# A decoder layer on one core: attention products moved one group later, one of the maxima products moved within its group

## The chip, the cores and the metric

The kernel runs on one core of a Trainium2 chip (trn2). The time is device microseconds of one execution, from launch to the last store; a measurement is repeated and its median given. The profile is of one execution of its own. Below, "us" is microseconds. PE is TensorE (matrix products), DVE is VectorE, ACT is ScalarE, POOL is GpSimd, SP is the engine that issues most DMAs here.

## The reference

Two sequences of 256 tokens, width 256 (512 tokens in all), pass through one decoder layer:

```python
x = layernorm(x + self_attention(x))        # 16 heads of 16, latents of 64, rotary half appended to q and k
x = layernorm(x + cross_attention(x, ctx))  # 16 heads, scores against 512 context rows of width 64
x = layernorm(x + moe(x))                   # 8 experts of 128, two per token, and a shared expert
```

The cross attention multiplies several weights of a head one after the other:

```python
q_hk  = (hidden_q @ Wq.T).reshape(b, s, H, K)
q_big = einsum('bshk,hkq->bshq', q_hk, w_kc_q)
q_r   = einsum('bshq,hqr->bhsr', q_big, W_qr)
k_r   = einsum('bld,hdr->bhlr', kv_rope, W_kr)
scores = einsum('bhsr,bhlr->bhsl', q_r, k_r)
```

The kernel multiplies these four weights with each other first, once for each head, so that a head's scores are x times one 256x64 matrix times the rotated context. These are the weight products that the change moves.

## The kernel before

All five engines run programs written out by hand; each engine executes its own list in order, and semaphores (`wait_ge`, `then_inc`) tie the lists together. What follows is about the first 70 us: the self attention.

**Groups.** The self attention is cut into 8 groups (`NGRP`), i = 0 to 7: four for each sequence, each of four heads (two pairs, pr = 0 and 1). The loop `for i in range(NGRP + 1): for j in range(4)` stands in the PE, ACT and DVE programs alike; a slot (i, j) says when a step is issued. For group i, in slots (i, 0) and (i, 2), PE computes the scores of a pair (`attn_max`, L587), DVE takes the row maxima (L1361), splits them in two parts (`max_split`, L1372 to L1376), PE transposes them (`attn_maxT`, L599, slot (i+1, 0)), and DVE adds them into the rows of `QS` (`max_rows`, L1383), which increments `mT_sb`. Two groups later PE computes the transposed scores (`attn_exp`, L613), ACT exponentiates (L1100); three groups later comes the product with the values (`attn_pv`, L629), four groups later the sum of the exponentials (`attn_sum`, L639) and on DVE its reciprocal (`attn_norm`, L1332 and L1335).

**Spread products.** Before group 2 (the heads of the third quad) can start, the operands `KS` and `QS` for pairs 4 to 7 are built: `late_stack(0)` to `late_stack(3)` (L548), in the slots `LATE_STACKS = [(0, 3), (1, 0), (1, 1), (1, 2)]`. All four write PSUM banks 2 and 3, so each waits until the one before is evacuated: 0 by ACT (KS, L1081), 1 by DVE (KS, L1300), 2 by ACT (QS, L1083), 3 by DVE (QS, L1302). The first `attn_max` of group 2 waits for all of them (`stack_act`, `stack_dve` at 4).

**Weight products.** For each of the 8 pairs of heads p (`NPAIR`) there are three steps on PE, each followed by an evacuation on ACT: E(p) (`step_E`, L681, 4 matmuls, loads as weights `wE`), G(p) (`step_G`, L694, 8 matmuls, needs E(p)), M(p) (`step_M`, L709, 8 matmuls, needs G(p)). Their slots come from `product_slots`; before the change they are:

```
group 0: E2 M0 | G1    | E3 M1 | G2        group 4:        |       | M6 | G7
group 1: E4 M2 | G3    | E5 M3 | G4        group 5:        |       | M7 |
group 2:       | E6    | M4    | G5
group 3:       | E7    | M5    | G6
```

M(p) and the transposed maxima of `attn_maxT` share PSUM bank 7. So `attn_maxT(i)` waits for the evacuations of the M before it (`M_out`), and M(p) waits for `max_rows` of the transpose before it (`mT_sb`). The weights of pairs 2g and 2g+1 come by three DMAs (`ld_wg[g]`); only E waits for them.

**Filler.** `keep_busy(n, 4)` issues n bf16 matmuls of 256 columns into bank 4 whose results nobody reads (L508). Group 1 has 8 of them in slot (1, 0) and 3 in each of (1, 1), (1, 2) and (1, 3).

**Next to it.** U products (`step_U`, L719) follow in slots (6, 1), (7, 1), (8, 0) and (8, 1); (6, 1) waits for all E evacuations. The output projection `attn_proj` in slot (7, 2) uses bank 6 after the last G. After group 8 come 18 rounds of cross attention and then the experts; they take M(p) from `M_sb`, and start after all M are evacuated.

Of the kernel before, what the change touches and what calls it, by code (L numbers as in the profile page):

```python
# [34 lines left out]
NPAIR = NH // 2  # L35
# [7 lines left out]
NGRP = 2 * NQUAD  # L43
# [5 lines left out]
def product_slots():  # L49
    slots = {}  # L50
    for p in range(NPAIR):
        fast = p < 4
        i, j = (p // 2, 2 * (p % 2)) if fast else (p - 2, 1)
        for step, q, at in [("E", p + 2, j), ("M", p, j if fast else j + 1), ("G", p + 1, j + 1 if fast else j + 2)]:
            if q < NPAIR:
                slots.setdefault((i, at), []).append((step, q))
    return slots


PRODUCTS = product_slots()  # L60
SH = 792
LAG = 2
# [6 lines left out]
def decoder_layer(nc, xT_in, pk_in, rope_in, spread_in, wE_in, wcT_in, wq_in, bv_up, xn_in, bo, wop_in, wu_in, sh_in,  # L69
                  kv_in, w13_in, w2_in, out):  # L70
    stack = ExitStack()
    with stack:
# [3 lines left out]
        def sem(name):  # L76
            return stack.enter_context(nc.semaphore(name))
# [140 lines left out]
        v_sb = sem("v_sb")  # L218
# [11 lines left out]
        mT_sb = sem("mT_sb")  # L230
# [13 lines left out]
        M_out = sem("M_out")  # L244
# [257 lines left out]
        def _(pe):  # L502
            def bank(k):
                return ps[:, k, :]

            def keep_busy(count, k):
                for _ in range(count):
                    pe.matmul(ps[:, k, 0:2 * P], busy[:, 0:P], busy[:], start=True, stop=True)  # L508
# [65 lines left out]
            def attn_max(i, pr):  # L574

                b, g = i // NQUAD, i % NQUAD
                n = 2 * i + pr
                if i in (0, 2) and pr == 0:
                    pe.wait_ge(stack_act, 2 + i)
                    pe.wait_ge(stack_dve, 2 + i)  # L580
                if n >= 1:
                    pe.wait_ge(max_sb, n)
                for u in range(2):
                    t = 2 * b + u
                    for par in range(2):
                        r = slice(64 * par, 64 * par + KROWS)
                        mm = pe.matmul(ps[:, par, u * SEQ:(u + 1) * SEQ], QS[r, 2 * g + pr, t * P:(t + 1) * P],  # L587
                                       KS[r, 2 * g + pr, b * SEQ:(b + 1) * SEQ], start=True, stop=True)
                mm.then_inc(max_ps, 1)

            def attn_maxT(i):

                if i == 0:
                    pe.wait_ge(consts, 2)
                pe.wait_ge(mpad_sb, i + 1)
                pe.wait_ge(M_out, 2 if i == 0 else min(NPAIR, i + 3))
                for pr in range(2):
                    for u in range(2):
                        mm = pe.transpose(ps[:, 7, pr * SEQ + u * P:pr * SEQ + (u + 1) * P], mpad[:, i % 2, u, pr, :], ident[:])  # L599
                mm.then_inc(mT_ps, 1)  # L600
# [97 lines left out]
            def step_M(p):  # L698

                pe.wait_ge(G_out, p + 1)  # L700
                if p == 0:
                    pe.wait_ge(rot_sin, 2)
                if p >= 1:
                    pe.wait_ge(M_out, p)
                if p in (2, 4, 5, 6, 7):
                    pe.wait_ge(mT_sb, max(1, p - 2))
                for c in range(2):
                    for k in range(2):
                        mm = pe.matmul(ps[:, 7, c * P + DC * k:c * P + DC * k + DC], wq[:, 2 * p + k, c * P:(c + 1) * P],  # L709
                                       G_sb[:, p % 2, DC * k:DC * k + DC], start=True, stop=True)  # L710
                mm.then_inc(M_ps, 1)
# [14 lines left out]
            step_G(0)  # L726
            for i in range(NGRP + 1):
                for j in range(4):
                    if i < NGRP and j % 2 == 0:
                        attn_max(i, j // 2)  # L730
                    if i >= ALAG and j % 2 == 0:
                        attn_exp(i - ALAG, j // 2)
                    if i >= 1 and j == 0:
                        attn_maxT(i - 1)
                    if (i, j) == (0, 2):
                        values(2)
                    if (i, j) in LATE_STACKS:
                        late_stack(LATE_STACKS.index((i, j)))
                    if i == 1:
                        if j == 0:  # L740
                            pe.wait_ge(v_sb, 2)
                        keep_busy(8 if j == 0 else 3, 4)
                    if i >= ALAG + 2 and j == 0:
                        attn_sum(i - ALAG - 2)
                    if i >= ALAG + 1 and j == 2:
                        attn_pv(i - ALAG - 1)
                    if i in (2, 3) and j == 1:
                        context_T(i - 2)
                    for step, p in PRODUCTS.get((i, j), []):
                        if step == "E":  # L750
                            step_E(p)
                        elif step == "M":
                            step_M(p)
                        else:
                            step_G(p)
                    if i == 6 and j == 1:
                        pe.wait_ge(E_out, NPAIR)
                        step_U(0, bank(5))
                    if i == 7 and j == 1:
                        pe.wait_ge(U_out, 1)  # L760
                        step_U(1, bank(5))
                    if i == 7 and j == 2:
                        pe.wait_ge(G_out, NPAIR)
                        attn_proj(0, ps[:, 6, 0:D], range(NQUAD))
                    if i == 7 and j == 3:
                        pe.wait_ge(U_out, 2)
                        attn_proj(1, ps[:, 5, 0:D], range(NQUAD))
                    if i == 8 and j < 2:
                        if j == 0:
                            pe.wait_ge(max_sb, 2 * NGRP)  # L770
                        step_U(2 + j, bank(j))
                    if i == 8 and j >= 2:
                        normed_T(0, x1, j - 2, 8 - j)
# [498 lines left out]
        def _(dve):  # L1272
# [24 lines left out]
            def stack_out(kq, count, pairs):  # L1297
                dve.wait_ge(stack_ps, count)
                if kq == 0:
                    v.tensor_scalar(KS[:, pairs, :], ps[:, 2:4, :], one_rows, None, ALU.add).then_inc(stack_dve, 1)  # L1300
                else:
                    v.tensor_copy(QS[:, pairs, :], ps[:, 2:4, :]).then_inc(stack_dve, 1)  # L1302
# [62 lines left out]
            def max_split(i):  # L1365

                dve.wait_ge(max_sb, 2 * i + 2)
                if i == 0:
                    dve.wait_ge(mpad_zero, 1)
                if i >= 2:  # L1370
                    dve.wait_ge(mT_ps, i - 1)
                v.tensor_copy(mhi[:, i % 2], mneg[:, i % 2]).then_inc(mhi_sb, 1)  # L1372
                dve.wait_ge(mhi_sb, i + 1)
                at = mpad[:, i % 2].rearrange("p u r (h c) -> p u (r h) c", h=2)
                v.tensor_copy(at[:, :, :, KROWS], mhi[:, i % 2].bitcast(F32))
                v.tensor_tensor(at[:, :, :, KROWS + 1], mneg[:, i % 2], mhi[:, i % 2].bitcast(F32), ALU.subtract).then_inc(mpad_sb, 1)  # L1376
# [8 lines left out]
            for i in range(NGRP + 1):  # L1385
                for j in range(4):
                    if i < NGRP and j % 2 == 0:
                        attn_max(i, j // 2)
                    if i == 0 and j in (0, 2):
                        values(j // 2)  # L1390
                    if i == 0 and j in (1, 2):
                        rotated_lo(j - 1)
                    if i >= 1 and j == 0:
                        max_rows(i - 1)
                    if (i, j) == LATE_STACKS[1]:
                        stack_out(0, 4, slice(6, 8))
                    if (i, j) == LATE_STACKS[3]:
                        stack_out(1, 6, slice(6, 8))
                    if i < NGRP and j == 2:
                        max_split(i)  # L1400
                    if i >= ALAG + 2 and j == 0:
                        attn_norm(i - ALAG - 2)
                    if i in (2, 3) and j == 1:
                        context_lo(i - 2)
                    if i == NGRP - 1 and j >= 2:
                        if j == 2:
                            dve.wait_ge(xbo, NT)
                        norm_stats(0, j - 2, ps[:, 8 - j, 0:D], x_nat)
                    if i == NGRP and j >= 2:
                        norm_apply(0, j - 2, x1)  # L1410
# [249 lines left out]
```

## Time and profile before

| what | value |
|---|---|
| time, median of 3 runs | 255.16 us (255.13 to 256.3) |
| time of the profiled execution | 255.44 us |
| its span, first to last instruction | 253.7 us |
| PE matmul busy | 238.6 us, 94% of the span |
| DVE busy | 194.2 us, 77% |
| ACT busy | 120.6 us, 48% |
| POOL busy | 119.8 us, 47% |
| TensorE clock granted, mean | 0.993 of full |

The span is the time between the first and last instruction of the profiled execution; what lies around it is 1.7 us. The busy share of PE counts overlapping records of a pipelined engine, so the time that a step takes of PE is better read from the distance between the start of its first matmul and the start of the next step.

### The profile page before, as it was taken

The page shows a single profiled execution, that of the slowest core. Times are in us where ns is not written, and L with a number is a line of the kernel's source. Part 1 is how long each engine was busy: PE and PEld are TensorE (multiplying, and loading weights), DVE is VectorE, ACT ScalarE, POOL GpSimd, SP SyncE. Part 2 cuts the span into 40 slices and gives each one's busy share as a digit, 9 for nine tenths or more (in the row PEclk, how much of TensorE's full clock was granted, in tenths as well). Part 3 has the DMA queues.
Part 4 walks back from the last instruction along what each step waited for, and adds up shares of the span by engine and source line. Part 5 has one row for each costly group of instructions (what it writes and reads, how often), then busy time and mean ns, then how long its engine had stood idle before and what let it go on. Part 6 is the DMA issues. An engine that isn't in the chain of part 4 may idle for free.

```text
span 253.7 us, 4411 instructions
## 1 busy us (share of the span) xinstructions
PE 238.6 (94%) x1581; PEld 172.7 (68%) x1581; DVE 194.2 (77%) x348; ACT 120.6 (48%) x253; POOL 119.8 (47%) x170
## 2 busy tenths in 40 slices
PE   7989999978999999999899999999999999999991
PEld 4468797755656557675667776668776777778870
DVE  1377578799874899769889999995857895886685
ACT  2555358655566355454366554454344434513360
POOL 7297300000025528757666666784465646502353
PEclk9999999999999999999999999999999999999997
DMA  6999970000000660000000000000000000000002
GB/s 240 331 268 264 402 281 0 4 1 3 0 3 1 123 125 3 0 0 0 4 0 0 4 0 0 4 0 0 3 0 0 0 4 0 0 3 0 0 3 83
DMA packets 4501, 13.66 MB, mean 54 GB/s; under 512 B 513, under 2 KB 1281, under 8 KB 4353
## 3 DMA queue, kind: packets, MB, share of 16 engines
q1 hardware_dynamic: 4048, 11.29, 13.8%
q0 software_dynamic: 432, 2.10, 3.8%
q8 instruction: 13, 0.21, 0.4%
q14 instruction: 8, 0.06, 0.1%
HBM read 14.43 MB, written 0.52 MB: 59 GB/s over the span
## 4 chain that ended last, share of the span: by engine, by line
PE 70%; DVE 16%; DMA 5%; issue 2%; ACT 2%; SPq 2%; POOL 1%; POOLq 0%
PE ps L854 10%; PE ps L807 6%; PE ps L868 5%; PE ps L834 5%; PE ps L835 5%; PE ps L808 5%; DMA wq<-in_wq 5%; PE ps L791 5%; DVE rcp L1332 3%; PE ps L934 3%; PE ps L647 3%; DVE mneg L1361 3%; PE ps L841 2%; DVE xmneg L1423 2%; PE ps L709 2%
## 5 line engine op out<-in xcount | busy, mean ns | idle before, releaser
L1195 ACT ACTIVATE probs<-ps 128x512 f32<-128x512 f32 x64 | 38.0, 597 | 57.0 <-PE ps L835 56.0
L1423 DVE TENSOR_REDUCE xmneg<-ps 128x1 f32<-128x512 f32 x64 | 43.1, 688 | 18.0 <-PE ps L808 17.7
L454 POOL TENSOR_TENSOR psums<-psums,probs 128x512 f32<-128x512 f32 x32 | 41.2, 1287 | 11.2 <-ACT probs L1195 8.5
L450 POOL TENSOR_TENSOR psums<-probs 128x512 f32<-128x512 f32 x16 | 20.5, 1281 | 34.2 <-ACT probs L1195 22.6
L807 PE MATMUL ps<-KA,QA 128*128 128x512 f32 x64 | 30.1, 470 | 2.1 <-DVE xmneg L1423 2.1
L854 PE MATMUL ps<-probs,kv_dup 128*64 128x256 f32 x256 | 31.1, 385 | 0.0
L1441 DVE RECIPROCAL xrcp<-ps 128x256 f32<-128x256 f32 x16 | 28.0, 1751 | 1.1 <-PE ps L841 1.0
L1361 DVE TENSOR_REDUCE mneg<-ps 128x4 f32<-128x1024 f32 x16 | 19.6, 1224 | 9.5 <-PE ps L587 9.1
L834 PE MATMUL ps<-QA,KA 128*128 128x512 f32 x64 | 26.0, 406 | 0.0
L398 POOL TENSOR_TENSOR rstd<-mv,eps_col 128x1 f32<-128x1 f32 x12 | 2.3, 188 | 49.5 <-DVE mv L1349 49.2
L835 PE MATMUL ps<-QB,KB 68*128 68x512 f32 x64 | 25.4, 397 | 0.0
L808 PE MATMUL ps<-KB,QB 68*128 68x512 f32 x64 | 25.3, 395 | 0.0
L854 PEld LDWEIGHTS ps<-probs,kv_dup 128*64 128x64 f32 x256 | 17.0, 136 | 11.2 <-ACT probs L1195 3.0
L1100 ACT ACTIVATE probs<-ps 128x512 f32<-128x512 f32 x32 | 17.3, 593 | 10.6 <-PE ps L613 10.5
L807 PEld LDWEIGHTS ps<-KA,QA 128*128 128x128 f32 x64 | 12.0, 188 | 11.8 <-DVE xmneg L1423 5.8
L791 PE MATMUL ps<-x1T,M_sb 128*128 128x256 f32 x64 | 16.4, 380 | 0.5 <-ACT x1T L1145 0.5
L868 PE MATMUL ps<-U_sb,ctxn 128*128 128x256 f32 x64 | 16.5, 380 | 0.2 <-DVE ctxn L1446 0.2
L1187 ACT ACTIVATE QA<-ps 64x256 fp32r<-64x256 f32 x32 | 12.1, 378 | 8.8 <-PE ps L791 8.4
L1416 DVE TENSOR_TENSOR QB<-ps,QA 64x256 fp32r<-64x256 f32 x32 | 13.3, 416 | 3.7 <-ACT QA L1187 3.2
L1223 ACT ACTIVATE QB<-ps,own_rows 4x256 fp32r<-4x256 f32 x32 | 13.1, 455 | 4.9 <-PE ps L818 4.6
L834 PEld LDWEIGHTS ps<-QA,KA 128*128 128x128 f32 x64 | 12.1, 190 | 3.3 <-issue 0.8
L1332 DVE RECIPROCAL rcp<-sums 128x256 f32<-128x256 f32 x8 | 14.0, 1748 | 0.3 <-ACT sums L1107 0.2
(163 smaller groups left out, 464.1 us busy)
## 6 DMA issues: line engine op xcount, KB each, us to landing
wu<-in_wu SPq DMA_DIRECT2D x4, 640.0 KB, 9.8
wq<-in_wq SPq DMA_DIRECT2D x4, 512.0 KB, 13.9
wcT<-in_wcT SPq DMA_DIRECT2D x4, 384.0 KB, 12.6
wE<-in_wE SPq DMA_DIRECT2D x4, 320.0 KB, 11.5
w13T<-in_w POOLq DMA_DIRECT2D x1, 1024.0 KB, 7.8
x1T<-in_xT SPq DMA_DIRECT2D x1, 512.0 KB, 3.7
kvp<-in_kv POOLq DMA_DIRECT2D x1, 512.0 KB, 6.1
x_nat<-in_xn SPq DMA_DIRECT2D x1, 512.0 KB, 19.6
```

Source lines behind the costliest of these rows:

```text
L454: g.tensor_tensor(psums[:, s, :], psums[:, s, :], probs[:, s, kc, :], ALU.add).then_inc(xadd_sb, 1)
L791: mm = pe.matmul(ps[:, query_bank(n), 0:SEQ], M_sb[:, c, p, :], x1T[:, c, b * SEQ:(b + 1) * SEQ], start=(c == 0), stop=(c == 1))
L807: pe.matmul(o, QA[:, s, hh, q], KA[:, b * LK:(b + 1) * LK], start=True, stop=False)
L808: pe.matmul(o, QB[:, s, hh, q], KB[:, b * LK:(b + 1) * LK], start=False, stop=True).then_inc(xmax_ps, 1)
L834: pe.matmul(o, KA[:, k0:k0 + P], QA[:, s, :, :], start=True, stop=False)
L835: pe.matmul(o, KB[:, k0:k0 + P], QB[:, s, :, :], start=False, stop=True).then_inc(xexp_ps, 1)
L854: mm = pe.matmul(ps[DC * hh:DC * hh + DC, 4 + n % 2, 0:SEQ], kv_dup[:, NKC * b + kc, 0, :], probs[:, n % 2, kc, hh * SEQ:(hh + 1) * SEQ], ...
L868: mm = pe.matmul(o, ctxn[:, p, t * P:(t + 1) * P], U_sb[:, p, :], start=(p == 0 and t < 2), stop=(p == NPAIR - 1))
L1195: a.activation(probs[:, n % 2, kc, :], ps[:, 2 + u % 2, :], ACT.Exp).then_inc(xexp_sb, 1)
L1361: v.tensor_reduce(mneg[:, i % 2, :, 2 * pr:2 * pr + 2].rearrange("p u h -> p h u"), ps[:, 0:2, :].rearrange("p h (u k) -> p h u k", u=2), ...
L1423: v.tensor_reduce(xmneg[:, n % 4, qt, hh:hh + 1], ps[:, u % 2, :], AX.X, ALU.max, negate=True).then_inc(xmax_sb, 1)
L1441: v.reciprocal(xrcp[:, n % 2, :], ps[:, 4 + n % 2, SEQ:2 * SEQ]).then_inc(xrcp_sb, 1)
```

## The change

The table of slots gets its slow pace from pair 3 on instead of pair 4:

```
group 0: E2 M0 | G1    | E3 M1 | G2        group 4:        | E7    | M5 | G6
group 1: E4 M2 | G3    |       |           group 5:        |       | M6 | G7
group 2:       | E5    | M3    | G4        group 6:        |       | M7 |
group 3:       | E6    | M4    | G5
```

The waits that keep bank 7 in order are adapted: `attn_maxT(i)` waits for M up to i+1, and M(p) from p = 2 on waits for `max_rows` of group p-2. The second `attn_max` of group 1 is issued in slot (1, 1), ahead of the third spread product `late_stack(2)`, instead of in slot (1, 2). The filler of group 1 is one call of 8 matmuls in slot (1, 3). On DVE `max_split` of a group stands ahead of the evacuation of the last spread product.

```diff
--- before.py
+++ after.py
@@ -49,8 +49,8 @@
 def product_slots():
     slots = {}
     for p in range(NPAIR):
-        fast = p < 4
-        i, j = (p // 2, 2 * (p % 2)) if fast else (p - 2, 1)
+        fast = p < 3
+        i, j = (p // 2, 2 * (p % 2)) if fast else (p - 1, 1)
         for step, q, at in [("E", p + 2, j), ("M", p, j if fast else j + 1), ("G", p + 1, j + 1 if fast else j + 2)]:
             if q < NPAIR:
                 slots.setdefault((i, at), []).append((step, q))
@@ -593,7 +593,7 @@
                 if i == 0:
                     pe.wait_ge(consts, 2)
                 pe.wait_ge(mpad_sb, i + 1)
-                pe.wait_ge(M_out, 2 if i == 0 else min(NPAIR, i + 3))
+                pe.wait_ge(M_out, min(NPAIR, i + 2))
                 for pr in range(2):
                     for u in range(2):
                         mm = pe.transpose(ps[:, 7, pr * SEQ + u * P:pr * SEQ + (u + 1) * P], mpad[:, i % 2, u, pr, :], ident[:])
@@ -702,8 +702,8 @@
                     pe.wait_ge(rot_sin, 2)
                 if p >= 1:
                     pe.wait_ge(M_out, p)
-                if p in (2, 4, 5, 6, 7):
-                    pe.wait_ge(mT_sb, max(1, p - 2))
+                if p >= 2:
+                    pe.wait_ge(mT_sb, p - 1)
                 for c in range(2):
                     for k in range(2):
                         mm = pe.matmul(ps[:, 7, c * P + DC * k:c * P + DC * k + DC], wq[:, 2 * p + k, c * P:(c + 1) * P],
@@ -726,8 +726,10 @@
             step_G(0)
             for i in range(NGRP + 1):
                 for j in range(4):
-                    if i < NGRP and j % 2 == 0:
+                    if i < NGRP and j % 2 == 0 and (i, j) != (1, 2):
                         attn_max(i, j // 2)
+                    if (i, j) == (1, 1):
+                        attn_max(1, 1)
                     if i >= ALAG and j % 2 == 0:
                         attn_exp(i - ALAG, j // 2)
                     if i >= 1 and j == 0:
@@ -736,10 +738,9 @@
                         values(2)
                     if (i, j) in LATE_STACKS:
                         late_stack(LATE_STACKS.index((i, j)))
-                    if i == 1:
-                        if j == 0:
-                            pe.wait_ge(v_sb, 2)
-                        keep_busy(8 if j == 0 else 3, 4)
+                    if (i, j) == (1, 3):
+                        pe.wait_ge(v_sb, 2)
+                        keep_busy(8, 4)
                     if i >= ALAG + 2 and j == 0:
                         attn_sum(i - ALAG - 2)
                     if i >= ALAG + 1 and j == 2:
@@ -1394,10 +1395,10 @@
                         max_rows(i - 1)
                     if (i, j) == LATE_STACKS[1]:
                         stack_out(0, 4, slice(6, 8))
+                    if i < NGRP and j == 2:
+                        max_split(i)
                     if (i, j) == LATE_STACKS[3]:
                         stack_out(1, 6, slice(6, 8))
-                    if i < NGRP and j == 2:
-                        max_split(i)
                     if i >= ALAG + 2 and j == 0:
                         attn_norm(i - ALAG - 2)
                     if i in (2, 3) and j == 1:
```

## Rows read from the trace of the kernel before

**Rows 1.** Chain of waits that ended last: start us, length us, what.
```profile
46.01 1.23 DVE mneg L1361
...
53.52 1.67 DVE rcp L1332
...
59.19 1.67 DVE rcp L1332
```

**Rows 2.** Timeline of PE, group 1: start us, us (first start to last end), what, idle before.
```profile
25.71 0.50 PE L548 MATMUL ps<-dhi,spread 32*128 32x512 f32 x2
...
26.38 1.05 PE L508 MATMUL ps<-busy 128*128 128x256 bf16 x8
27.26 0.60 PE L681 MATMUL ps<-wE 128*96 128x128 f32 x4
27.70 1.00 PE L709 MATMUL ps<-resid,wq 128*128 128x64 f32 x8
28.63 0.50 PE L548 MATMUL ps<-dhi,spread 32*128 32x512 f32 x2
...
30.57 0.50 PE L587 MATMUL ps<-KS,QS 48*128 48x256 f32 x4
31.00 0.50 PE L548 MATMUL ps<-dhi,spread 32*128 32x512 f32 x2
...
32.43 1.00 PE L709 MATMUL ps<-resid,wq 128*128 128x64 f32 x8
33.27 0.49 PE L508 MATMUL ps<-busy 128*128 128x256 bf16 x3
33.60 1.00 PE L694 MATMUL ps<-resid,wcT 96*128 96x64 f32 x8
34.53 0.50 PE L587 MATMUL ps<-KS,QS 48*128 48x256 f32 x4
```

**Rows 3.** Timelines of DVE and then ACT, group 1.
```profile
26.38 0.68 DVE L1383 TENSOR_TENSOR QS<-ps,QS 128x512 fp32r<-128x512 f32 x1
26.98 1.27 DVE L1300 TENSOR_SCALAR KS<-ps,pk 128x1024 fp32r<-128x1024 f32 x1
...
32.25 1.22 DVE L1302 CAST QS<-ps 128x1024 fp32r<-128x1024 f32 x1
...
29.40 1.02 ACT L1083 ACTIVATE QS<-ps 128x1024 fp32r<-128x1024 f32 x1 [0.28 <-PE ps L548]
```

**Rows 4.** Timeline of the DMA queue of SP, and the landing times of the wq transfers.
```profile
7.36 0.43 SPq L312 DMA_DIRECT2D wq<-in_wq x1
...
DMA to landing us min/median/max: 8.2/13.9/18.8
```

**Rows 5.** Timeline of PE, groups 4 to 7.
```profile
46.63 0.60 PE L639 MATMUL ps<-CT,sel 128*128 128x256 f32 x2
47.30 0.50 PE L587 MATMUL ps<-KS,QS 48*128 48x256 f32 x4
...
49.91 1.06 PE L694 MATMUL ps<-resid,wcT 96*128 96x64 f32 x8
51.15 0.50 PE L587 MATMUL ps<-KS,QS 48*128 48x256 f32 x4 [0.18 <-DVE mneg L1361]
...
54.64 1.10 PE L709 MATMUL ps<-resid,wq 128*128 128x64 f32 x8
56.83 0.50 PE L587 MATMUL ps<-KS,QS 48*128 48x256 f32 x4 [1.08 <-DVE mneg L1361]
...
60.20 1.07 PE L629 MATMUL ps<-probs,V 128*32 128x256 f32 x16
62.50 0.50 PE L587 MATMUL ps<-KS,QS 48*128 48x256 f32 x4 [1.23 <-DVE mneg L1361]
```

**Rows 6.** Stretches: bounds us, length, busy us (count) by engine, PEclk granted, DMA share, GB/s.
```profile
56.80:62.50 5.70, 4.45 (x46) 2.67 (x47) 5.48 (x9) 3.41 (x7) 0.00 (x0) 1.00 0.01 3
250.00:253.70 3.70, 0.00 (x0) 0.00 (x0) 1.09 (x2) 0.00 (x0) 0.85 (x3) 0.51 0.22 73
```

## The prediction

> **What bounds the kernel now.** I read the page first, then the chain of waits in order of time, then the timelines of PE, DVE and ACT over the self attention, and last the stretches with the granted clock. The chain shows two regimes. Up to about 46 us nearly every piece of it is a PE piece. From there on it runs through DVE: the maxima at 46.01, then one reciprocal per group, at 53.52 and 59.19, so a group takes 59.19 - 53.52 = 5.67 us whatever PE does [rows 1]. The timeline of PE says the same: in group 1 no row between 25.71 and 34.53 has idle time before it, so each step there pushes the next [rows 2]; in groups 5 and 6 PE sits idle for 1.08 and 1.23 us until DVE has read the scores (56.83 and 62.50) [rows 5]. Work taken off PE in groups 1 to 3 can therefore bring its full length; work put on PE in groups 5 and 6 is free up to about a microsecond each. That is the argument; what follows is whether the waits let it through.
>
> **What is taken from group 1.** I take the PE time of a step as the distance to the next start. E: 27.70 - 27.26 = 0.44. M followed by filler, as M3 is: 33.27 - 32.43 = 0.84; M followed by real work: 28.63 - 27.70 = 0.93. G: 34.53 - 33.60 = 0.93. Three fillers: 33.60 - 33.27 = 0.33; eight: 27.26 - 26.38 = 0.88. A late spread product: 26.38 - 25.71 = 0.67. A maxima product: 31.00 - 30.57 = 0.43 [rows 2]. Group 1 loses E5 (0.44), M3 (0.84), G4 (0.93) and nine of 17 fillers (3 x 0.33 = 0.99): 3.20 us. This is the most the change can bring in group 1.
>
> **What waits appear in it.** I walk group 1 from 26.38, where the second spread product ends and nothing has changed yet.
> - E4 starts at 26.38 and not at 27.26, and ends its slot at 26.82. Its weights must be there: the last of the three transfers of this pair of pairs is issued at 7.36, and even with the longest landing time of the four, 18.8, it is there at 26.2 [rows 4].
> - M2 now waits for `max_rows(0)` on DVE, 26.38 + 0.68 = 27.06 [rows 3]; with a few hundredths for the signal it starts at 27.10. That is the first new wait, 0.28. Slot end 28.03.
> - The second maxima product, 28.03 to 28.46; it waits for the first one's reduction, which is over before `max_rows(0)` begins.
> - The third spread product at 28.46 (the KS evacuation it waits for ends at 26.98 + 1.27 = 28.25 [rows 3]). ACT begins the evacuation 29.40 - 28.63 = 0.77 after the product starts and takes 1.02 [rows 2, 3]: 29.23 to 30.25.
> - G3 from 29.13 to 30.06. The fourth spread product needs ACT's evacuation: 30.30, a second wait of 0.24. DVE evacuates it from 30.30 + 0.77 = 31.07, for 1.22 [rows 3], to 32.29. DVE is free by then: the reduction, 1.23 by [rows 1], starts at about 28.6 and the three tiny instructions of the split follow.
> - The eight fillers end their slot at 30.30 + 0.67 + 0.88 = 31.85. The first maxima product of group 2 waits for DVE: 32.35, a third wait of 0.50.
>
> Group 2 starts at 32.35 in place of 34.53 [rows 2]: 2.18 us earlier. The cross sum agrees: 3.20 - 0.28 - 0.24 - 0.50 = 2.18. The bounds: no waits would give 3.20. If each of the four hand-overs (DVE to PE, PE to ACT, ACT to PE, PE to DVE to PE) took 0.1 more than I allow, it is 1.8.
>
> **Groups 2 and 3** hold the same kinds of steps as before, with p one lower (E5 for E6, M3 for M4, G4 for G5, and so on), and the same waits between them; all of them move together. I cost this at nothing, since as much work leaves each of these groups as enters it. No DMA is issued by a moved step. The queue of SP isn't touched; the U weights and the expert weights come from other places in it and are first needed in group 6.
>
> **Group 4** gets E7 in slot (4, 1) (before, it had no E). Before, the sum product ends at 46.63 + 0.60 = 47.23 and the second maxima product starts at 47.30, when DVE has done the first maxima (46.01 + 1.23 = 47.24) [rows 1, 5]. In the old times E7 runs 47.23 to 47.67 and pushes all behind it by 0.37. The last step of the group (G6 in place of G7) then starts at 49.91 + 0.37 = 50.28 and its slot ends at 51.21; before, the next group's maxima product started at 51.15, released by DVE [rows 5]. DVE takes the product at once, so this loss of 0.06 goes to the end of the kernel. With the full record of G (1.06) it is 0.19. I take 0.10.
>
> **Group 5** gets G7 behind M6. From 54.64 + 0.10: M 0.93, G 0.93, slot end 56.60. DVE releases the next maxima product at 56.83 + 0.10 = 56.93 [rows 5]. Hidden, with 0.33 to spare; with the full records (1.10 and 1.06) it ends at 56.90, just inside. **Group 6** gets M7 behind the product with the values: 60.20 + 0.10 + 1.07 = 61.37, slot end 62.30, full record 62.47, and DVE releases at 62.60 [rows 5]. Hidden again. M7 must also be evacuated before `attn_maxT(6)`; that transpose comes after a maxima product (0.43) and a scores product of group 7, and the evacuation is one ACT instruction over half the columns of the 1.02 one [rows 3]. The cover of both is DVE's 5.67 us per group; if it were gone, G7 and M7 would cost 0.93 each. From group 7 on nothing is changed, and everything there hangs on semaphores of this program, so the shift reaches the end.
>
> **The sum.** 2.18 - 0.10 = 2.1 us. The profiled span would go from 253.7 to 251.6 and the profiled execution from 255.44 to 253.3. That execution lay 0.28 above the median of the runs; against the median, 255.16 - 2.1 = 253.1 us, 0.8% less. What this measurement can tell from no change is about 0.5%, or 1.28 us.
>
> **The rivals.**
> - *A, the forecast:* gain 1.4 to 2.6 us, 252.6 to 253.8. Lower end: hand-overs of 1.8 and the full 0.4 of near misses in groups 4 to 6; upper end: half of the three waits not there. Chance 0.72.
> - *B, the moved products come back in the DVE-bound groups.* For it: three steps are added there, and the spare time is thin (0.33 and 0.30 us). If E7, G7 and M7 all lay on the path, 0.44 + 0.93 + 0.93 = 2.30 us would be paid back and the time would be 255.3; if half of it does, 254.1. Against it: the two idle times of 1.08 and 1.23 us are long enough for a step of 0.93 each [rows 5]. Chance 0.15, of which 0.11 ends within 0.5%.
> - *C, the waits in group 1 are longer, so that the chain of spread products and evacuations, not PE, sets its length.* It does already in my walk (third wait). If the evacuation of the third spread product on ACT came 1 us late, behind other evacuations, the gain would be 1.1 and the time 254.1. Against it: ACT has only E4 and M2 to evacuate before it. Chance 0.04, within 0.5%.
> - *D, the gain is larger,* 2.6 to 3.2 us (252.0 to 252.6): the waits overlap with what is modelled as PE time. Chance 0.04.
> - *E, slower: the clock of TensorE falls in groups 1 to 3,* where nine fillers are gone and three waits appear. Every microsecond of full-speed work takes two at the lower of the two levels (1.2 against 2.4 GHz). From the second wait, 30.30, to the start of group 4, 43.3 (its first maxima product stands 0.5, the record of such a product, ahead of the reduction at 46.01, less 2.2 [rows 1, 2]), lie 13 us of PE-bound work: all of it at the lower level gives 253.1 + 13 = 266 us; 2.1 + 1.28 = 3.4 us of it suffices to be slower by over 0.5%. Against it: a stretch without any filler, 56.80 to 62.50, with 4.45 us busy of 5.70 and a wait of 1.23, was granted 1.00, and the only stretch with a low grant (0.51) is the last 3.7 us, where PE did nothing [rows 5, 6]. The new waits are half a microsecond at most. Chance 0.05.
>
> The Trainium skill speaks for E: its page "TensorE: Matmul & The Clock Gate", section "A second HAM failure mode: psum-queue depth-cycling", says that a PE which idles briefly and often between groups of matmuls, as it cycles through PSUM banks, can swing between the two clock levels. By it this kernel would lose its clock in group 1 and more so in groups 5 and 6, which wait longer and hold no filler. This trace does not agree, since those groups were granted 1.00.
>
> **How the numbers follow.** Faster by over 0.5%: A and D whole and 0.04 of B, 0.80. Within 0.5%: 0.11 of B and C, 0.15. Slower: E, 0.05. The predicted time is A's, 253.1. The range of 252.3 to 254.5 reaches over A into D and to the half-paid case of B and to C; it leaves out E, the full B and the far end of D, under 2 in 10.
>
> **What would show it.** In the profile after: E4 at 26.4 and M2 at about 27.1 with a short wait for DVE L1383; the fourth spread product at about 30.3, released by ACT; the first maxima product of group 2 at 32.3 to 32.5, released by DVE L1302; group 4's first at 43.3 to 43.5; the idle time before the maxima products of groups 6 and 7 shrunk from 1.08 and 1.23 to about 0.3 each, still ended by DVE; reciprocals still 5.67 apart; a granted clock of 1.00 throughout. The prediction is wrong if group 2 starts later than 33.2 (C), if the idle time before those two products is zero and reciprocals are more than 5.7 apart (B), or if a stretch before 50 us has a clock under 1 (E).

## The result and the profile after

| what | before | after |
|---|---|---|
| median of 20 executions | 255.46 us | 254.16 us |
| fastest execution | 255.13 us | 253.17 us |
| ratio, 95% interval | 1 | 0.996 [0.9941, 0.998] |
| profiled execution, its span | 255.44, 253.7 us | 256.40, 254.6 us |
| mean granted clock in it | 0.993 | 0.982 |

The change is faster by 0.4%, half of the 0.8% that were forecast. The median is a poor description of it: the 20 executions are of two kinds. Eleven have a mean granted clock of 0.993 or more and take 253.17 to 254.26 us; nine have 0.987 or less and take 255.03 to 265.76 us. The profiled one is of the second kind. The ratio leaves out two executions that were far off, while the counts below take all of them. Below, an execution has "lapsed" where its mean clock is 0.990 or less, and its clock is "held" otherwise; "the fall" is the moment at which the granted clock goes from 1.00 to 0.50.

The stretches of the changed kernel, columns as in [rows 6]:

```profile
24.00:30.60 6.60, 6.45 (x48) 4.84 (x48) 5.25 (x9) 3.03 (x5) 2.87 (x6) 1.00 1.01 387
30.60:37.40 6.80, 6.72 (x33) 4.91 (x32) 3.98 (x6) 1.99 (x5) 0.77 (x2) 0.50 0.74 295
37.40:64.00 26.60, 25.76 (x260) 19.93 (x258) 22.89 (x37) 18.18 (x42) 0.00 (x0) 1.00 0.01 2
```

For 6.8 us the grant is 0.50, the lower level of 1.2 GHz. It falls at 30.66 us, at the second of the new waits. The timeline of PE in the same execution, against [rows 2] and [rows 5]:

```profile
26.60 0.68 PE L681 MATMUL ps<-wE 128*96 128x128 f32 x4
27.42 1.07 PE L709 MATMUL ps<-resid,wq 128*128 128x64 f32 x8
28.43 0.50 PE L587 MATMUL ps<-KS,QS 48*128 48x256 f32 x4
...
29.52 1.10 PE L694 MATMUL ps<-resid,wcT 96*128 96x64 f32 x8
30.70 0.79 PE L548 MATMUL ps<-dhi,spread 32*128 32x512 f32 x2
31.30 0.62 PE L548 MATMUL ps<-dlo,spread 32*128 32x512 f32 x2
31.85 1.89 PE L508 MATMUL ps<-busy 128*128 128x256 bf16 x8
33.67 0.79 PE L587 MATMUL ps<-KS,QS 48*128 48x256 f32 x4
...
40.16 0.50 PE L587 MATMUL ps<-KS,QS 48*128 48x256 f32 x4
...
57.76 0.50 PE L587 MATMUL ps<-KS,QS 48*128 48x256 f32 x4 [0.18 <-DVE mneg L1362]
...
63.43 0.50 PE L587 MATMUL ps<-KS,QS 48*128 48x256 f32 x4 [0.20 <-DVE mneg L1362]
```

Read it from the top. E4 comes directly after the spread product; M2 comes 0.82 later where E takes 0.44, because of the wait for `max_rows(0)` (first new wait, 0.38); the fourth spread product comes 1.18 after G3 where G takes 0.94, because of the wait for ACT (second new wait, 0.24), and from there each record is longer: the pair of spread records 0.79 and 0.62 where [rows 2] has 0.50, eight fillers 1.82 to the next start against 0.88. Below, G7 and M7 have filled the idle time before the first maxima products of groups 6 and 7: 1.08 and 1.23 in [rows 5], 0.18 and 0.20 now. DVE still ends both.

### The profile page after: what moved, and what is told of

It is laid out like the page before. It is cut to its first block, busy times and chain, and to the rows that moved or that the text cites. A ratio compares the mean times of both kernels' runs of the same rounds, so it can differ in the third digit from the quotient of the medians.

```text
span 254.6 us, 4393 instructions
## 1 busy us (share of the span) xinstructions
PE 242.2 (95%) x1572; PEld 174.8 (69%) x1572; DVE 195.5 (77%) x348; ACT 120.9 (47%) x253; POOL 119.9 (47%) x170
## 4 chain that ended last, share of the span: by engine, by line
PE 77%; DVE 15%; ACT 3%; issue 2%; POOL 1%; POOLq 0%
PE ps L855 10%; PE ps L808 6%; PE ps L869 5%; PE ps L835 5%; PE ps L836 5%; PE ps L809 5%; PE ps L792 5%; PE ps L935 3%; PE ps L647 3%; PE ps L508 3%; DVE rcp L1333 3%; PE ps L587 2%; PE ps L842 2%; DVE xmneg L1424 2%; PE ps L709 2%
```

## The experiments

Fifteen runs follow: eleven new kernels, and again the change, the kernel before and (twice) the second of the new ones. Executions of the kernel before were taken beside them in four sets, 97 in all. Two theories went in. Theory 1: the schedule saves what was predicted, and the clock takes a part back in some executions. Theory 2: the clock is noise common to all versions, and the schedule saves less than predicted.

**Filler back where it was.**
```diff
-                    if (i, j) == (1, 3):
-                        pe.wait_ge(v_sb, 2)
-                        keep_busy(8, 4)
+                    if i == 1:
+                        if j == 0:
+                            pe.wait_ge(v_sb, 2)
+                        keep_busy(8 if j == 0 else 3, 4)
```


> The change, with the 17 filler matmuls of group 1 back where they were (8 in slot (1, 0), 3 in each of the other three). Theory 1 (the products moved save what was predicted, but with the emptier group 1 the TensorE clock falls in a part of the executions, as in the profile of the changed kernel from 30.7 to 37.4 us): with the filler the clock holds; the fillers cost 0.7 us of the gain, since the walk of group 1 then ends at 33.0 in place of 32.35, so about 253.9 us in every execution, with none near 256. Theory 2 (the low clock in that profile is chance and as frequent in any version; the smaller gain comes from waits or from groups 4 to 6): executions scatter as those of the change do, 253.9 to 257, median about 255.

Median 254.03 us (ratio 0.9933 [0.9908, 0.9958]). Ten of 12 executions took 253.64 to 254.42 us; two had a clock of 0.987, at 255.5. So there were fewer lapses (2 of 12 against 9 of 20, a difference that chance could still give), though not none as expected, and the fillers cost some 0.5 us of time. The profiled execution held its clock, so where the two lapsed is not shown.

**Filler in the waits.** The 2 + 2 fillers stand where PE waits, and 12 where it waits for DVE's last evacuation.
```diff
                         elif step == "M":
+                            if (i, j) == (1, 0):
+                                pe.wait_ge(v_sb, 2)
+                                keep_busy(2, 4)
                             step_M(p)
...
+                    if (i, j) == (1, 2):
+                        keep_busy(2, 4)
                     if (i, j) in LATE_STACKS:
...
-                        keep_busy(8, 4)
+                        keep_busy(12, 4)
```


> The change, with filler put into its three new waits: 2 before M2, 2 before the fourth spread product, 12 in place of 8 in slot (1, 3); 16 in all. Theory 1: the clock holds, and since the filler lies in idle time the time is 253.2 us in all executions, 0.9% under before: it beats both kernels. Theory 2: no different from the change, median 254.2 with executions at 256 to 256.6.

Median 253.77 us, ratio 0.9918 [0.9891, 0.9945], six executions from 253.22 to 254.06, clock 0.992 to 0.999. Two further sets of executions follow below.

**The filler edit alone, in the kernel before.** The same diff as the first one, read backwards, applied to the kernel before.

> The kernel before with only the filler edit of the change: 8 in slot (1, 3), none in the other slots of group 1; all products where they were. Theory 1 in the form that missing filler alone makes the clock fall: executions near 254.5 (0.99 us of filler gone from the path, 0.3 us of a new wait before M2) mixed with others 2 to 3 us above. Theory 1 in the form that the waits of the change are needed for it: 254.5 us throughout. Theory 2: 254.5 with the scatter of the kernel before.

Eight of 12 executions took 254.78 to 255.32 us with the clock held; four lapsed, one at 255.87 us and three at 260.82, 273.31 and 273.66, with clocks of 0.976, 0.924 and 0.925. Among the 97 executions of the kernel before, one was as late as these three (271.51). So the moved filler alone seems to be enough for a long lapse; the profiled execution held its clock, so where it falls is not shown. Held, this kernel is some 0.4 us under the kernel before: that part of the whole gain is filler that is no longer on the path.

**No filler in group 1.**
```diff
-                    if (i, j) == (1, 3):
-                        pe.wait_ge(v_sb, 2)
-                        keep_busy(8, 4)
```


> The change without any filler in group 1. The eight fillers lie in the wait for DVE, so with the clock held the time is that of the change's best executions, 253.1 us. Theory 1: the clock falls in more executions than with the eight, median 256 or more. Theory 2: as the change, median 254.2.

All 12 executions had a lapse: 254.8 to 260.7 us, median 257.56. Five had clocks of 0.989 or 0.990, one 0.984 and six 0.967, so the lapses are of different lengths. The profiled one was at 0.50 for 13.6 us, from 31.6, while PE waited for DVE (no row of PE between 30.83 and 32.19):

```profile
24.00:31.70 7.70, 6.59 (x48) 4.52 (x46) 6.02 (x9) 2.73 (x6) 3.09 (x5) 0.99 1.02 408
31.70:45.20 13.50, 13.01 (x68) 11.70 (x70) 7.12 (x11) 6.57 (x14) 0.00 (x0) 0.50 0.21 83
45.20:64.00 18.80, 18.55 (x194) 13.90 (x196) 16.16 (x24) 12.24 (x30) 0.00 (x0) 1.00 0.01 2
```

This settles theory 2 in its first half: the lapses depend on the filler. They go from 12 of 12 without any to 9 of 20 with eight to none of 6 with some in the waits.

**Filler in the waits, again.** The same kernel.

> The same kernel as fill_waits, for more executions of it. Theory 1 (enough PE work in the waits holds the clock): executions between 253.2 and 254.1 us, mean clock 0.992 and above, hardly any at 255 or more. Rival (the six executions so far were luck): a third or more of them at 0.982 and 256 us, as with the change.

Five of six took 253.26 to 253.68 us; one took 266.25 with a clock of 0.942. The change has two of this kind (265.24 and 265.76, 0.943) and the kernel before one (271.51, 0.939). So the version doesn't exclude lapses, and whether it makes this rare kind rarer is not shown.

**Twelve late fillers.** `keep_busy(8, 4)` in slot (1, 3) becomes `keep_busy(12, 4)`, nothing in the waits.

> The change with 12 in place of 8 filler matmuls in slot (1, 3) and none in the two earlier waits. In the profile of the change the clock fell at 30.7 us, before the filler of slot (1, 3) begins at 31.85. Theory 1a (what matters is PE's work before that point, so filler behind it is too late): mixed executions as the change, 40% at 255 us and above. Theory 1b (what matters is the amount over the whole of group 1): clearly fewer of them than the 9 of 20 of the change, time 253.2 to 254. The four more lie in the wait for DVE and cost nothing.

Five of 12 lapsed (255.84 to 257.07 us), about the share of the change. Its profiled execution held the clock and is the one to compare the walk with:

```profile
26.20 0.68 PE L681 MATMUL ps<-wE 128*96 128x128 f32 x4
27.04 1.08 PE L709 MATMUL ps<-resid,wq 128*128 128x64 f32 x8 [0.16 <-DVE QS L1384]
28.04 0.50 PE L587 MATMUL ps<-KS,QS 48*128 48x256 f32 x4
28.47 0.50 PE L548 MATMUL ps<-dhi,spread 32*128 32x512 f32 x2
...
29.14 1.10 PE L694 MATMUL ps<-resid,wcT 96*128 96x64 f32 x8
30.32 0.49 PE L548 MATMUL ps<-dhi,spread 32*128 32x512 f32 x2
...
32.42 0.51 PE L587 MATMUL ps<-KS,QS 48*128 48x256 f32 x4
...
37.16 0.50 PE L587 MATMUL ps<-KS,QS 48*128 48x256 f32 x4
...
43.36 0.51 PE L587 MATMUL ps<-KS,QS 48*128 48x256 f32 x4
...
49.08 0.50 PE L587 MATMUL ps<-KS,QS 48*128 48x256 f32 x4
...
60.44 0.50 PE L587 MATMUL ps<-KS,QS 48*128 48x256 f32 x4 [0.20 <-DVE mneg L1362]
```

**The same number, placed in the waits.** 2 before M2, 2 before the fourth spread product, 8 in slot (1, 3).

> The change with 2 filler matmuls before M2, 2 before the fourth spread product, and the 8 of slot (1, 3): as many as in the kernel with 12 late ones, otherwise placed. Theory 1a: the clock holds as with the 16, 253.2 to 254.1 us. Theory 1b: the same mixture as with 12 late ones.

None of six lapsed, 253.31 to 253.85 us. With the total of 12 equal, this speaks for the place of the filler (1a) and against its amount in group 1 (1b); but none of six against five of 12 could still be chance. What carries it is the sum over all runs: with filler in both waits (12 or 16 in all, whole change) 1 of 24 executions lapsed, with 8 or 12 behind them 20 of 44.

**The move of the weight products alone,** with the filler of the version above that has 16.
```diff
-                    if i < NGRP and j % 2 == 0 and (i, j) != (1, 2):
+                    if i < NGRP and j % 2 == 0:
                         attn_max(i, j // 2)
-                    if (i, j) == (1, 1):
-                        attn_max(1, 1)
...
-                    if i < NGRP and j == 2:
-                        max_split(i)
                     if (i, j) == LATE_STACKS[3]:
                         stack_out(1, 6, slice(6, 8))
+                    if i < NGRP and j == 2:
+                        max_split(i)
```


> The move of the weight products alone: the second maxima product of group 1 back in slot (1, 2) behind the third spread product, the split on DVE back behind the last evacuation; filler as in fill_waits, so that the clock should hold. By the walk with the lengths of fill_waits the third spread product starts 0.4 us earlier, but DVE then has the reduction of 1.23 us ahead of the last evacuation, and group 2 starts 0.2 us later than there: 253.5 us, so the moved products bring 1.7 of the 1.9 us and the maxima product with the split 0.2. Rival: the order of the maxima product is worth its whole reduction, 1.2 us, and the time is 254.5.

253.52 to 253.98 us, median 253.68, none of six lapsed. E4 starts at 26.05 and the first maxima product of group 2 at 32.67: 6.62, against 6.29 with the whole change and the same filler (26.04 and 32.33). The maxima product with the split is worth 0.3 us in the profile, and the spans of the fastest executions, 251.8 and 251.4, say the same. The medians don't resolve it: 253.68 here, 253.77, 253.55 and 253.64 in three sets with the whole change. The rival's 1.2 is out.

**The kernel before with another profile.**

> The kernel before, once more with a profile. In 20 of its 46 executions beside the experiments the mean clock was 0.990 or less and the time 1.1 us or more above the others, while the profile shown had 1.00 in every stretch up to 250 us. If this profile catches such an execution, theory 1 expects the low stretch in group 1 or 2, between 26 and 40 us; the rival expects it elsewhere (start or end of the program), so that it has nothing to do with these edits.

255.38 us and 1.00 throughout; no lapse was caught.

**The maxima product and the split alone, in the kernel before.** The diff of the move alone, read backwards, on the kernel before, with its own filler.

> The kernel before with only the second part of the change: the second maxima product of group 1 ahead of the third spread product, and the split ahead of the last evacuation on DVE. All products and all 17 filler matmuls as before. PE stays without idle time up to group 2 by the walk (the evacuations are ready by 30.9 and 33.0, when PE needs them at 31.0 and 34.5), so no change: 255.2 us where the clock holds. Rival: DVE's earlier reduction lets the later steps start earlier, 254.5.

Ten of the 12 executions held the clock; leaving out one of them at 592.6 us (the kernel before had one at 592.79; the cause is not known), they took 254.99 to 255.40. Ratio 0.9986 [0.9969, 1.0002]: nothing, as the walk says. Its profiled execution had a lapse (clock 0.989, 256.16 us), and it is not in group 1:

```profile
45.00:57.50 12.50, 11.11 (x114) 8.19 (x113) 10.98 (x17) 7.07 (x17) 0.00 (x0) 1.00 0.01 3
57.50:61.80 4.30, 4.30 (x26) 2.48 (x22) 3.69 (x4) 1.92 (x4) 0.00 (x0) 0.60 0.02 4
61.80:80.00 18.20, 17.19 (x145) 11.13 (x142) 13.30 (x26) 10.64 (x25) 2.62 (x7) 1.00 0.00 1
```

The products of groups 4 to 6 stand here as in the kernel before. The grant is 0.50 from 57.7 to 61.1 us, and falls 0.8 us after PE has resumed behind the idle time between groups 5 and 6:

```profile
56.89 0.51 PE L587 MATMUL ps<-KS,QS 48*128 48x256 f32 x4 [1.08 <-DVE mneg L1363]
...
57.56 1.04 PE L599 MATMUL ps<-ident,mpad 128*128 128x128 f32 x4
58.39 1.06 PE L639 MATMUL ps<-CT,sel 128*128 128x256 f32 x2
59.38 1.91 PE L719 MATMUL ps<-wu 128*64 128x256 f32 x8
```

Its mean clock and time are those of most lapsed executions of the kernel before: 24 of the 97 have 0.989 or 0.990 and 256.09 to 256.50 us. Eight more have 0.987 or less.

**Two fillers in one of the two waits only,** 8 in slot (1, 3) in both.

> The change with 2 filler matmuls in its first new wait only (before M2), 8 in slot (1, 3). If any added PE work ahead of 30.7 us holds the clock: no execution above 255. If the second wait, just ahead of the point where the clock fell in the profile, is what counts: the same mixture as the change, 40% above 255. Time with the clock held 253.2 to 254.1 in both.

> The change with 2 filler matmuls in its second new wait only (before the fourth spread product), 8 in slot (1, 3). If the second wait is what counts, the clock holds in all executions, 253.2 to 254.1 us; if the sum of PE's work ahead of it counts, this and the version with 2 before M2 do about equally, between the change (9 of 20 above 255) and the version with both (none of 6).

With the first wait filled, five of 12 lapsed (256.64 to 265.97 us). With the second filled, two of 11 lapsed by the mean (256.78 and 256.85), and two more at 254.79 and 255.14 had spans of 1.4 us above the fastest; the profile of one of these shows a short lapse, 0.52 from 30.2 to 33.6 us. So four of 11, and a mean clock above 0.990 doesn't exclude a short lapse. Neither wait alone is enough. Nor is the second wait needed for the fall. With that wait filled, the clock falls at 30.35 us, as its filler begins and with no wait since M2; with the first filled, at 30.78, when the second wait ends. Filler and stretches of the kernel with the second wait filled, then stretches of the one with the first wait filled:

```profile
30.35 0.62 PE L508 MATMUL ps<-busy 128*128 128x256 bf16 x2
...
30.00:30.50 0.50, 0.50 (x6) 0.48 (x6) 0.43 (x3) 0.50 (x1) 0.43 (x1) 0.85 1.00 410
30.50:31.00 0.50, 0.50 (x5) 0.11 (x2) 0.24 (x2) 0.32 (x2) 0.00 (x0) 0.50 1.06 430
```

```profile
30.00:30.50 0.50, 0.50 (x7) 0.50 (x5) 0.44 (x2) 0.50 (x1) 0.00 (x0) 1.00 1.03 420
30.50:31.00 0.50, 0.41 (x4) 0.28 (x5) 0.25 (x2) 0.50 (x2) 0.00 (x0) 0.78 1.03 420
```

**Idle time of groups 5 and 6 filled, in the kernel before.**
```diff
+                    if i in (5, 6) and j == 3:
+                        pe.wait_ge(G_out, NPAIR)
+                        ones = ident[:].bitcast(BF16)
+                        for _ in range(8):
+                            pe.matmul(ps[:, 6, 0:2 * P], ones[:, 0:P], ones, start=True, stop=True)
                     if i >= ALAG + 2 and j == 0:
```


> The kernel before with 8 filler matmuls more in slot (5, 3) and in slot (6, 3), into bank 6, in the idle time of 1.08 and 1.23 us that the change fills with G7 and M7. If the executions of the kernel before at 256.2 us (20 of 46 in two sessions) come from a clock that falls there: none of them is left, all at 255.0 to 255.5. If they come from elsewhere: a third or more at 256.2 still.

The fillers stand where PE was idle; its waits for DVE shrink from 1.08 and 1.23 us to 0.20 and 0.25:

```profile
55.35 1.04 PE L747 MATMUL ps<-ident 128*128 128x256 bf16 x8
56.59 0.50 PE L587 MATMUL ps<-KS,QS 48*128 48x256 f32 x4 [0.20 <-DVE mneg L1366]
...
60.97 1.05 PE L747 MATMUL ps<-ident 128*128 128x256 bf16 x8
62.26 0.50 PE L587 MATMUL ps<-KS,QS 48*128 48x256 f32 x4 [0.25 <-DVE mneg L1366]
```

None of 12 executions lapsed (clock 0.992 to 0.998), ten at 255.13 to 255.64 and two at 256.0 without a low clock. The kernel before itself lapsed in 4 of 23 executions beside it, at 256.2 to 256.3, and in 32 of 97 over all four sets of runs. None of 12 against 4 of 23 could be chance, against 32 of 97 hardly. The median does not move (0.9999 [0.9986, 1.0012]); no execution with a low clock, 1.1 us late, is among the 12.

**The change and the version with filler, side by side.** The unchanged kernels.

> The change itself once more. Theory: two kinds of executions, 253.2 to 254.1 with a mean clock above 0.99, and 255 to 257 with one at 0.98 or so, in about 6 and 4 of 10; the former 1.9 us under the undisturbed ones of the kernel before. Rival: all alike near 254.2.

> The change with filler in its three waits (2, 2, 12) once more, beside the change in the same session. Theory: at most one execution in ten above 255, median 253.6, against 4 in 10 of the change.

The change: six of 12 at 253.44 to 254.01 us, six at 256.08 to 258.04 with clocks of 0.973 and 0.982; median 255.05, ratio 0.9983 [0.9953, 1.0013]. Taken alone, these 12 can't be told from no change. With filler in the waits: 253.27 to 253.95, none of six lapsed, median 253.64, ratio 0.9929 [0.9913, 0.9946].

## Why the prediction was wrong, and what in it held

**The walk held.** The prediction was wrong in its term for the clock, which it put at nothing; its sum over the waits was close. Where the clock held, the walk can be laid beside the profile with 12 late fillers step by step, from the start of E4:

| from E4 to | forecast | measured | before |
|---|---|---|---|
| M2 | 0.72 | 0.84 | |
| second maxima product | 1.65 | 1.84 | |
| third spread product | 2.08 | 2.27 | |
| fourth spread product | 3.92 | 4.12 | |
| group 2 | 5.97 | 6.22 | 8.15 [rows 2] |
| group 7 | 34.04 | 34.24 | 36.12 [rows 2, 5] |

(The "before" column counts from 26.38, where the spread product ends.) Group 1 saves 8.15 - 6.22 = 1.93 in place of 2.18. What was mis-sized is the hand-over: M2 starts 0.12 later after the wait than I allowed, and takes 1.00 of PE to the next step where I had 0.93. The lower bound of 1.8 held. In group 4, E7 lengthened the distance to group 5 to 49.08 - 43.36 = 5.72, against 51.15 - 45.47 = 5.68 before (45.47: the first maxima product, 0.54 ahead of the reduction of [rows 1]); 0.04 in place of 0.10. G7 and M7 cost nothing: the idle time shrank to about 0.2 where I had 0.3, and the reciprocals stayed 5.68 apart (51.37, 57.05 and 62.73 in that profile). At group 7 the gain is 1.88. Spans agree: the fastest execution of the change has 251.4 us, the fastest of the kernel before 253.2. B and C are out, and with them theory 2 in its second half, that the schedule saves less.

**The clock was the step that failed.** The sum has no term for it: I expected a granted clock of 1.00 throughout, gave E 0.05, and made it a matter of slower or not. By the prediction's own sign, a stretch before 50 us with a clock under 1, it was wrong. The clock lapsed in 15 of 32 executions of the change: eleven of them at 0.982 like the two that were profiled, one at 0.987, one at 0.973 and two at 0.943. Its price in the profiled one: from E4 to the first maxima product of group 3 it took 40.16 - 26.60 = 13.56, with the clock held 37.16 - 26.20 = 10.96. So 6.8 us at the lower level cost 2.6, more than the schedule saves; such an execution is slower than the kernel before with its clock held. The mean over both kinds is what remained of the gain. In E I had counted that 3.4 us of full-speed work, done at the lower level, would cost 3.4 us; 6.8 us at 0.50 hold about that much work and cost 2.6, since part of it hid in the third wait (group 2 starts 33.67 - 26.60 = 7.07 after E4, 0.85 later than with the clock held). So the price was near, and the chance was wrong.

**Luck.** The median of 254.16 lies in the stated range, but not for its reasons. Held executions lie around 253.5, most lapsed ones around 256.3, and the median falls between them because 9 of 20 lapsed. In the later set, with 6 of 12, it was 255.05, outside the range.

**Why I put the chance wrong.** My evidence was one stretch, 56.80 to 62.50, granted 1.00 in spite of a wait of 1.23 and no filler [rows 5, 6]. That was one execution. The kernel before itself seems to lapse there in others. No profile caught it, but a kernel with the same products in groups 4 to 6 was caught, at 0.60 on the mean from 57.5 to 61.8 us, and with that idle time filled none of 12 executions lapsed, against 32 of 97. The page "TensorE: Matmul & The Clock Gate" of the Trainium skill, section "A second HAM failure mode: psum-queue depth-cycling", which I set against this trace, tells of another kernel in which PE idles briefly between groups of matmuls and the clock swings. The falls measured here agree with it in that: at 30.66 us after waits of 0.38 and 0.24 us, at 57.7 after one of 1.08. They differ from my reading that one profile had refuted it. That the cycling through PSUM banks plays a part is not shown by any run.

**What the change does, then,** is three things: it takes 1.9 us off group 1 (0.3 of it by the order of the maxima product); it removes, as far as the filled kernel shows, a lapse of 1.1 us that the kernel before has in a quarter of its executions (24 of 97), by putting G7 and M7 where PE was idle; and it creates a lapse of about 2.6 us in over a third of them (11 of 32) by leaving group 1 emptier ahead of 30.7 us. With fillers in the two waits the third was not seen again: 17 of 18 executions of the version with 16 fillers lay between 253.22 and 254.06 us, medians 253.77, 253.55 and 253.64, ratios 0.9918, 0.9907 and 0.9929 to the kernel before. That version beats both kernels.

**Left open.** The place where the clock falls was seen in six profiles, not in every lapsed execution: that the 0.98 executions of the change all lapse in group 1 is inferred from two profiles of it and from the effect of the filler. Two fillers in each of two places were enough for that; how few would do, and why an execution lapses or not with the same kernel, was not settled. The origin of the rare executions at 0.92 to 0.94 (265 to 274 us), in which the kernel before shares, was not looked into; no profile caught one. The spans of held executions of the versions with filler in both waits scatter by 0.9 us (251.4 to 252.3); in the profiles this goes with the start of E4, 25.98 to 26.72, so with work before it; which, was not tested. The times scatter for another reason as well. What lies outside the span is 1.7 to 1.8 us in all 97 executions of the kernel before and in all 18 with 16 fillers, but 2.1 to 2.4 in 14 of 32 of the change and in nine of 12 with twelve late fillers, and up to 3.6 without filler. So a median of times holds up to some tenths that no step of the schedule explains; no trace shows where they come from.

## What to carry to other kernels

Filler matmuls are part of a schedule: an edit that takes them away or moves them behind a wait has to be costed as a chance of a lower clock, with its price read from the PE-bound work that follows. One profile with a clock of 1.00 shows that the clock can hold over that stretch, not that it does; compare the mean granted clock of all executions before using a stretch as evidence. When an edit opens a wait on PE, try filler in the wait itself. Here four matmuls in the two waits cost 0.07 us (group 2 starts 6.29 after E4 with them, 6.22 without), while four more behind the waits did not lower the share of lapses by anything that 12 executions can show.

## What the runs showed of the hardware

In the changed kernel the clock fell after two waits of 0.38 and 0.24 us, by the distances between starts. PE is recorded busy for 6.45 of the 6.6 us ahead of the fall (24.0 to 30.6), and still the grant went to 0.50. In the kernel with filler in the first wait alone it is recorded busy for 6.70 of 6.70 us (24.0 to 30.7), and the grant fell at 30.78; the record of G3 (1.10) reaches over most of the second wait. So the busy share that a profile shows for PE does not tell whether its clock will hold.

Four small bf16 matmuls of about 0.11 us each in the two waits went with 1 lapsed execution of 24 (12 or 16 fillers, whole change), against 15 of 32 without them. The work there is fp32 products with 32, 48 or 96 of 128 rows and 64-column outputs; whether that matters was not tested. The low stretches that the profiles show lasted about 3.4 us (twice), 6.8 (three times) and 13.6.
